# First stage of a gated stack on one core: the lower products move into the next cycle

## The reference

```python
def _smooth_quant_linear(x, w):
    s = sqrt(max(amax_over_rows(x), EPS) / max(amax_over_rows(w), EPS)); s = max(s, EPS)
    xs, ws = x / s, w * s
    x_scale = max(amax_over_columns(xs), EPS) / 127
    w_scale = max(amax_over_columns(ws), EPS) / 127
    return round(xs / x_scale) @ round(ws / w_scale).T * x_scale * w_scale.T

gate, up = split(_smooth_quant_linear(layernorm(x), fside), 2)     # upper: 512 -> 512
a = silu(gate) * up
x = x + tanh(g) * _smooth_quant_linear(a, ctx)                     # lower: 256 -> 512
```

## Time and profile before

| | |
|---|---|
| median of three runs | 1310.73 us |
| the profiled execution | 1311.2 us |
| its span | 1309.5 us |
| PE busy in the span | 1169.4 us (89%) |
| DVE busy | 831.5 us (63%) |
| ACT busy | 661.6 us (51%) |
| POOL busy | 398.6 us (30%) |
| mean granted TensorE clock | 0.964 |
| first stage ends, next one's first rows | 222.4 us |

### The profile page before, as it was taken

The page is one execution under the profiler, slowest core; times in us unless marked ns, Lnnn a source line. Parts: engine busy times, 40 slices in busy tenths (PEclk is TensorE's granted clock), DMA queues, the critical chain, the costliest instruction groups (busy, mean ns, idle before and its releaser), DMA issues.

```text
span 1309.5 us, 16528 instructions
## 1 busy us (share of the span) xinstructions
PE 1169.4 (89%) x5292; PEld 508.2 (39%) x5293; DVE 831.5 (63%) x1292; ACT 661.6 (51%) x1157; POOL 398.6 (30%) x465
## 2 busy tenths in 40 slices
...
GB/s 244 126 105 137 49 97 159 226 211 161 192 146 156 149 148 135 54 255 196 90 48 139 128 126 94 79 77 83 75 82 82 79 81 61 50 1 9 33 41 49
DMA packets 111893, 145.79 MB, mean 111 GB/s; under 512 B 25048, under 2 KB 79832, under 8 KB 111560
## 3 DMA queue, kind: packets, MB, share of 16 engines
...
## 4 chain that ended last, share of the span: by engine, by line
PE 33%; DVE 10%; issue 7%; ACT 5%; POOL 1%; DMA 1%; ACTq 0%; POOLq 0%; DVEq 0%
PE PS L2902 7%; PE PS L2803 5%; PE PS L2868 5%; PE PS L2887 4%; DVE a_top L3263 4%; PE PS L2827 3%; PE PS L2387 2%; ACT shared_w L3023 2%; ACT a_E L3023 2%; PE PS L2410 1%; PE PS L1980 1%; PE PS L2014 1%; POOL a_K L2147 1%; DMA a_rows<-f_y,l_pos 1%; PE PS L2815 0%
## 5 line engine op out<-in xcount | busy, mean ns | idle before, releaser
L3263 DVE TENSOR_REDUCE a_top<-PS 128x2 f32<-128x1024 f32 x256 | 309.3, 1222 | 88.4 <-PE PS L2887 84.9
L2868 PE MATMUL PS<-a_Q,a_K 99*128 99x512 bf16 (+1 forms) x512 | 166.2, 386 | 15.1 <-ACT a_E L3023 3.2
L3023 ACT ACTIVATE shared_w<-PS 128x512 f32<-128x512 f32 x256 | 138.8, 596 | 74.7 <-PE PS L2868 74.6
L3023 ACT ACTIVATE a_E<-PS 128x512 f32<-128x512 f32 x256 | 138.9, 596 | 63.7 <-PE PS L2868 63.5
L1498 PE MATMUL PS<-f_W,f_GT 128*128 x312 | 142.2, 599 | 0.2 <-ACT f_GT L1532 0.2
L2887 PE MATMUL PS<-a_K,a_Q 64*128 64x512 bf16 x512 | 100.5, 390 | 7.9 <-DVE a_top L3263 6.4
L1927 POOL TENSOR_TENSOR a_qf<-a_qf,a_tab 128x512 f32<-128x512 f32 x15 | 19.1, 1270 | 286.4 <-DVE a_swapped L3165 286.4
L2868 PEld LDWEIGHTS PS<-a_Q,a_K 99*128 99x128 bf16 (+1 forms) x512 | 44.1, 97 | 150.1 <-ACT a_E L3023 51.1
L1554 DVE TENSOR_TENSOR f_H<-f_SG,PS 128x256 f32<-128x256 f32 x39 | 16.4, 421 | 115.5 <-ACT f_SG L1538 115.5
L1498 PEld LDWEIGHTS PS<-f_W,f_GT 128*128 128x128 f32 x312 | 56.9, 192 | 57.9 <-issue 57.9
L2803 PE MATMUL PS<-a_xT,a_early 128*128 128x512 f32 x128 | 72.9, 667 | 2.0 <-ACT a_xT L2989 0.7
...
## 6 DMA issues: line engine op xcount, KB each, us to landing
f0r_raw<-in_L_ffn_W_dram SPq DMA_DIRECT2D x24, 512.0 KB, 5.3
...
v_units<-V SPq DMA_DIRECT2D x16, 512.0 KB, 2.9
a_V<-v_units SPq DMA_DIRECT2D x16, 512.0 KB, 3.6
...
```

The costliest lines, as they stand in the source:

```text
L2868: nc.tensor.matmul(PS[:, 4 + h % 2, :], K6[k][0:rows_, o, head // 2, kt * P:(kt + 1) * P], Q6[k][0:rows_, o, head // 2, :], start=True, st ...
L3023: nc.scalar.activation(E[step % 2][:, h, :], PS[:, 4 + h % 2, :], ACT.Exp).then_inc(exp_done, 1)
L3263: nc.vector.tensor_reduce(top[:, h - h % 2:h - h % 2 + 2, t], PS[:, 2 * pair:2 * pair + 2, :], AX.X, ALU.max).then_inc(maxed, 1)
```

## The change

The lower products and outputs of a batch move one cycle on: cycle `i` now runs the upper linear of batch `u = i`, the front of the lower linear of `d = i - 1` (turns, scales, rounded turns), and the products and outputs of batch `e = i - 2`. Within the cycle:

- TensorE no longer turns `dw` between the halves of `guw`; `dw` and `a` are turned together after the upper rows and side slot 2. The upper products follow the lower weights' rounded turns, and the lower x's rounded turns come after them. Three lower products of `e` stand behind the turns of `xh`, the fourth behind slot 1.
- VectorE takes `y` out between the ratio and the gates, runs the gates ahead of the fourth `y`, and takes the lower linear's scales in smaller pieces. 
- ScalarE runs the sines and the angles' copy at the end of a cycle, then `xqT_down`, silu and a root (of the next batch's deviation, or a spare one of a constant where there is none) ahead of the upper root. The norm of the next x moves forward, between the lower linear's steps.
- GpSimd adds a batch two cycles after its upper linear.
- `FILL` holds 8, 7, 7, 7 and 11 jobs instead of 8, 7, 7, 8 and 10, none in slot 7; the angles' job moves from slot 1 of its own cycle to slot 7 of the cycle before it.

The fourth lower product of each batch gets another bank. The diff, cut to the loops:

```diff
-        DOWN_AT = (4, 5, 6, 0)
-        LAST_AT = (0, 1, 2, 5)
+        DOWN_AT = {b: (4, 5, 6, 4) for b in range(NB - 2)}
+        DOWN_AT[NB - 2] = (4, 5, 6, 2)
+        DOWN_AT[NB - 1] = (0, 1, 2, 5)
...
+    if b >= 2:
+        add_batch(b - 2)
+    if b == NB - 1:
+        add_batch(NB - 2)
...
+def lower_products(d, tiles):
+    for t in tiles:
+        product(down, t, DOWN_AT[d][t])
...
-    u, d = i, i - 1
+    u, d, e = i, i - 1, i - 2
     pe.wait_ge(up.w_loaded, 16 * (u + 1))
     if u:
         pe.wait_ge(hs_ready, u * TB)
     turn_w(up, u, 1, 2)
-    if d >= 0:
-        pe.wait_ge(down.w_loaded, 16 * (d + 1))
-        if d:
-            pe.wait_ge(y_ready, d * TB - 2)
-        turn_w(down, d, 0, 4)
-        if d:
-            pe.wait_ge(y_ready, d * TB)
     turn_w(up, u, 0, 0)
     if u == 0:
         side.tensor_start(pe)
...
     turn_x(up, u, 1, 2)
     pe.wait_ge(up.reduced, 4 * u + 2)
     turn_x(up, u, 0, 0)
+    if e >= 0:
+        pe.wait_ge(down.xqT_ready, e + 1)
+        lower_products(e, (0, 1, 2))
     side.tensor(pe, i, 1)
-    if d >= 0:
-        turn_down_x(d)
+    if e >= 0:
+        pe.wait_ge(y_ready, e * TB + 1)
+        lower_products(e, (3,))
     s_rows(up, u, (0, 0), (1, 0))
     side.tensor(pe, i, 2)
     if d >= 0:
-        s_rows(down, d, (6, 0), (6, 256))
+        pe.wait_ge(down.w_loaded, 16 * (d + 1))
+        if d:
+            pe.wait_ge(y_ready, d * TB)
+        turn_w(down, d, 0, 4)
+        turn_down_x(d, 4)
     side.tensor(pe, i, 3)
     wsc_row(up, u, 1)
     side.tensor(pe, i, 4)
+    pe.wait_ge(up.w_shifted, u + 1)
+    turn_shifted(up.ws, 0, (2, 3), up.wqT_done)
+    if d >= 0:
+        s_rows(down, d, (6, 0), (6, 256))
     side.tensor(pe, i, 5)
+    pe.wait_ge(up.wsc_row_ready, u + 1)
+    pe.wait_ge(up.x_scaled, u + 1)
+    turn_shifted(up.ws, 1, (0, 1), up.wqT_done)
+    pe.wait_ge(up.x_shifted, u + 1)
+    for half, banks in ((0, (2, 3)), (1, (0, 1))):
+        pe.wait_ge(up.wqT_ready, 2 * u + half + 1)
+        turn_shifted(up.xs, half, banks, up.xqT_done)
     if d >= 0:
         wsc_row(down, d, 4)
-    finish_up(u)
-    side.tensor(pe, i, 6)
-    if d >= 0:
-        finish_down(d)
+        turn_down_ws(d)
     pe.wait_ge(up.xqT_ready, 2 * u + 2)
     for t in range(TB):
         product(up, t, t)
+    side.tensor(pe, i, 6)
     if d >= 0:
-        pe.wait_ge(down.xqT_ready, d + 1)
-        for t in range(TB - 1):
-            product(down, t, DOWN_AT[t])
+        turn_down_xs(d)
     side.tensor(pe, i, 7)
-    if d >= 0:
-        pe.wait_ge(hs_ready, u * TB + 1)
-        product(down, TB - 1, DOWN_AT[TB - 1])
-
...
+def bring_root():
+    nc.scalar.activation(spare_root[:], ln_eps[:], ACT.Sqrt)
...
     if d >= 0:
-        side.scalar(act, d, 7)
-        side.scalar_waves(act, d)
         silu(d)
-    side.scalar(act, i, 0)
-    side.scalar(act, i, 1)
-    root(up, u)
-    if d >= 0:
-        root(down, d)
         if u < NB - 1:
             norm_root(u + 1)
+        else:
+            bring_root()
+    side.scalar(act, i, 0)
+    root(up, u)
+    side.scalar(act, i, 1)
     side.scalar(act, i, 2)
     side.scalar(act, i, 3)
     shift_w(up, u)
     take_wsc_row(up, u, 1)
+    if d >= 0:
+        root(down, d)
     side.scalar(act, i, 4)
+    take_up_w(u, 0, 2)
     shift_x(up, u)
     if u == 0:
         norm_root(1)
+    take_up_w(u, 1, 0)
     side.scalar(act, i, 5)
-    take_up_w(u)
     if d >= 0:
         shift_w(down, d)
         take_wsc_row(down, d, 4)
-        shift_x(down, d)
-    side.scalar(act, i, 6)
+    if 0 < u < NB - 1:
+        normalize(u + 1)
     if d >= 0:
         take_down_w(d)
-        take_down_x(d)
-    if u < NB - 1:
-        normalize(u + 1)
+        shift_x(down, d)
     if u == 0:
         act.wait_ge(gates_loaded, 32)
         nc.scalar.activation(tg[:], gates[:], ACT.Tanh).then_inc(tg_ready, 1)
+        normalize(1)
+    side.scalar(act, i, 6)
+    if u < NB - 1:
+        side.scalar_waves(act, u)
+        side.scalar(act, i, 7)
+    if d >= 0:
+        take_down_x(d)
 d = NB - 1
+silu(d)
+bring_root()
 side.scalar(act, d, 7)
-silu(d)
...
-    u, d = i, i - 1
+    u, d, e = i, i - 1, i - 2
     reduce_turned(up, u, 0, 2)
-    if d >= 0:
-        reduce_turned(down, d, 0, 4)
     reduce_turned(up, u, 1, 0)
     v.wait_ge(up.x_ready, u + 1)
     reduce_turned(up, u, 2, 2)
     reduce_turned(up, u, 3, 0)
+    ratio(up, u)
+    if e >= 0:
+        take_down(e, (0, 1))
+    s_columns(up, u)
+    if e >= 0:
+        take_down(e, (2,))
+    if u == 1:
+        row_stats(3)
     if d >= 0:
         gate(d)
-    ratio(up, u)
-    s_columns(up, u)
+    if e >= 0:
+        take_down(e, (3,))
+    scale_w(up, u, 1, 0)
+    if d >= 0:
+        reduce_turned(down, d, 0, 4)
+    w_scales(up, u)
     if d >= 0:
         reduce_turned(down, d, 1, 4)
         ratio(down, d)
-    scale_w(up, u, 1, 0)
+    scale_x(up, u, 0, 0)
     if d >= 0:
         s_columns(down, d)
-    w_scales(up, u)
-    x_scales(up, u, 0, 0)
+    x_scales(up, u)
+    if 0 < u < NB - 1:
+        row_shifts(u + 1)
     if d >= 0:
         v.wait_ge(down.x_ready, (d + 1) * TB)
         scale_w(down, d, 6, 256)
         w_scales(down, d)
-        x_scales(down, d, 6, 0)
+    if u == 0:
+        v.wait_ge(x_loaded[1], 16)
+        row_stats(1)
+    take_up_x(u)
+    if u == 0:
+        row_shifts(1)
+    if d >= 0:
+        scale_x(down, d, 6, 0)
+        x_scales(down, d)
         if d == 0:
             v.wait_ge(tg_ready, 1)
         gate_scale(d)
-    if u == 0:
-        v.wait_ge(x_loaded[1], 16)
-        row_stats(1)
-    if u == 1:
-        row_stats(3)
-    if 0 < u < NB - 1:
-        row_shifts(u + 1)
-    take_up_x(u)
-    if u == 0:
-        row_shifts(1)
     take_up(u)
     if u == 0:
         row_stats(2)
-    if d >= 0:
-        take_down(d, False)
-d = NB - 1
-reduce_turned(down, d, 0, 4)
+d, e = NB - 1, NB - 2
+reduce_turned(down, d, 0, 0)
+take_down(e, (0, 1, 2))
...
-    ANGLES = 1
-    FILL = ((2, 0, 1, 0, 1, 1, 1, 2), (0, 1, 1, 1, 1, 1, 1, 1), (0, 1, 1, 1, 1, 1, 1, 1), (0, 1, 1, 1, 1, 1, 1, 2),
-(2, 1, 1, 1, 2, 1, 2, 0))
+    ANGLES = ((0, 1), (0, 7), (1, 7), (2, 7))
+    FILL = ((2, 0, 1, 1, 2, 1, 1, 0), (0, 1, 2, 1, 1, 1, 1, 0), (0, 1, 2, 1, 1, 1, 1, 0), (0, 1, 2, 1, 1, 1, 1, 0),
+(2, 1, 1, 1, 2, 2, 2, 0))
     WAVES = 17
 
```

More of the change, by code:

```diff
@@ L415, in shift_x, with take_up_w @@
                 last.then_inc(L.x_shifted, 1)
-            def take_up_w(u):
-                for half, bank in ((0, 2), (1, 0)):
-                    act.wait_ge(up.wqT_done, 2 * u + half + 1)
-                    nc.scalar.activation(up.wqT[:, 2 * half:2 * half + 2, :], PS[:, bank:bank + 2, :], ACT.Copy,
-                                         bias=-ROUNDER).then_inc(up.wqT_ready, 1)
+            def take_up_w(u, half, bank):
+                act.wait_ge(up.wqT_done, 2 * u + half + 1)
+                nc.scalar.activation(up.wqT[:, 2 * half:2 * half + 2, :], PS[:, bank:bank + 2, :], ACT.Copy,
+                                     bias=-ROUNDER).then_inc(up.wqT_ready, 1)
             def take_down_w(d):
@@ L607, in take_down @@
                     v.wait_ge(x_updated, b * TB)
-                for t in range(TB):
+                for t in tiles:
                     v.wait_ge(down.product_done, b * TB + t + 1)
-                    nc.vector.scalar_tensor_tensor(y[:, t, :], PS[:, (LAST_AT if last else DOWN_AT)[t], :], gated_scale[:, t:t + 1], down.wsc_row[:],
+                    nc.vector.scalar_tensor_tensor(y[:, t, :], PS[:, DOWN_AT[b][t], :], gated_scale[:, t:t + 1], down.wsc_row[:],
                                                    ALU.mult, ALU.mult).then_inc(y_ready, 1)
-                    if last and t:
-                        add_rows(b, t - 1)
-                if last:
-                    add_rows(b, TB - 1)
             def add_rows(b, t):
```

72 lines of the change are left out of this document (33 added, 39 removed).

## The result

Changed kernel: median 1295.87 us (1290.46 to 1297.79), run beside the kernel before at 1310.44 (1309.64 to 1312.04): ratio 0.9879, 95% interval 0.9852 to 0.9905. The forecast was 1298.7. The profiled execution was the lowest of the runs, 1290.46 (span 1288.6). Two more series gave medians of 1293.3 and 1296.3 (ratios 0.9869 and 0.9876). The change makes the kernel 1.2% to 1.3% shorter, and none of the three intervals reaches 1.

What follows compares the result with a forecast made beforehand. No engine was full; VectorE, the fullest, had 23.9 us of removable waits in the first stage. Waits -14.1, cycle 0 +1.1, tail +0.2, port +2.1 and -1.3 sum to -12.0: 1298.7 us, range 1292.5 to 1306.5.

Steps and rivals of the forecast that it cites:

- Cycle 0: +1.1: Later xs_up shift less a side product moved away: net +1.1 us, bounds 0 (TensorE at its higher level) and 4.
- some 4 us later: Cycle 0, ScalarE: the shift of xs_up stands behind more side copies and half of wqT_up, some 4 us later.
- the returned waits: New VectorE waits in cycles 2 and 3: guw's turn 2.6, dw's turn 1.5, turned x 0.3, together 4.4 us.
- the first rival: Gates beside GpSimd's angles pay the port in full, 3.5 us in each of three cycles: 1307.1 us; chance 0.08.
- The term of +2.1: Gates slowed by sharing the port with GpSimd's angles: 0.7 us in each of three cycles.
- Tail: +0.2: Turned a reduced 8.6 instead of 10.0 us after hs, an extra side job costing 1.7: +0.2 us (-1.4 to +1.7).
- the root's wait: VectorE's old wait of 2.70 us in each cycle for ScalarE's root; covered in cycles 2 and 3, 0.7 left in cycle 1.
- the wait on the products: VectorE's old waits of 6.45 us in cycle 2 and 4.66 in cycle 3 for the upper products, forecast to go.
- the cover of the root: Cycles 2 and 3: VectorE's two y run until the root is there, with 0.5 us to spare.
- the loop's terms: Slower rival: sines waiting for GpSimd's angles close a loop of 34.5 us, against a cycle of 41; 1316 us, chance 0.05.
- TensorE's lower level: Rival: turns and first products at 1.2 GHz behind waits, 3 us uncovered in each of three cycles: 1307.7 us; chance 0.08.
- ScalarE's loads: Rival: three table loads ahead of the root, each 1.28 us dearer, +10.4 us: 1309.1, no change; chance 0.03.

Runs made afterwards that it cites:

- e1: The changed kernel run again without any edit; median 1293.3 us, ratio 0.9869 to the kernel before.
- e12: The changed kernel run once more without any edit, on the chip of the three kernels before it; median 1296.3 us, ratio 0.9876.
- e6: The changed kernel with the old table of side jobs in cycle 0; median 1301.2 us, ratio 0.9903 to the kernel before.
- e10: The changed kernel with GpSimd's angles held until the cycle's gates are done and the tail's gates ahead of the lower outputs; 1293.2 us, ratio 0.9861.
- e7: The changed kernel with the tail's four gates ahead of all lower outputs; median 1296.3 us, ratio 0.9879 to the kernel before.
- e2: The kernel before with only the upper products moved ahead of the lower turns of ws and xs; median 1316.8 us, ratio 1.0066.
- e5: The kernel before with upper products ahead of the lower turns, and the root and its table ahead of slot 1's copy; 1316.5 us, ratio 1.0040.
- e4: The changed kernel with the turns of the lower xs put back ahead of the upper products; median 1313.3 us, ratio 1.0024 to the kernel before.
- e9: The changed kernel with lower products and outputs put back into their own cycle; median 1301.6 us, ratio 0.9915 to the kernel before.

## Why the prediction was right, and where its terms were not

The sum of -12.0 stands against -16.9 in the profiled stage (-13.5 and -19.8 in e1 and e12) and -14.6, -16.4 and -16.4 in the medians. That the total is so close is in part luck: cycle 0 was forecast 4.5 us too long and the tail 3.8 too short, and these two errors cancel. By its own split (waits, gates and small operations of each cycle together), predicted and measured in the first profile:

- Cycle 0: +1.1, measured -3.4. The step that failed is the shift of `xs_up`, "some 4 us later": ScalarE began it at 33.69, not 33.39, 1.0 us further behind its scale, as the further copies fitted into the idle 1.09 and 0.36 ahead of it. With half of `wqT_up` taken before it, TensorE turned xs at 36.28 instead of 38.00, and the product of 2.72 between turn and products was gone. e6 shows that the side-job table had no part in it. A second part was not in the sum: 1.4 of the 3.4 us is busy time of VectorE. The angles' copy now stands behind the root, GpSimd starts its angles at 21.77 instead of 20.94, and four small operations that took 0.44, 0.43, 0.32 and 0.72 take 0.17, 0.21, 0.17 and 0.16. TensorE also stayed at its higher level, the case for which the prediction had put 0 (granted clock 1.00 in 28 to 41 us, 0.79 before). Cycle 0 is the largest error. TensorE before, then ScalarE and TensorE after:

```profile
38.00 2.82 PE L283 MATMUL PS<-identf,xs_up 128*128 128x128 f32 x16 [2.13 <-ACT wqT_up L420]
```

```profile
33.69 2.55 ACT L417 ACTIVATE xs_up<-xs_up,inv_scale_up 128x512 f32<-128x512 f32 x4
```

```profile
36.28 2.19 PE L291 MATMUL PS<-identf,xs_up 128*128 128x128 f32 x16 [0.96 <-ACT xs_up L417]
```

- Cycle 1: -4.9, measured -5.3. Cycle 2: -5.2, measured -6.8: the returned waits are 3.65 + 1.17 = 4.8 (forecast 4.4), but `hs` is 0.6 shorter and the gates are only 0.4 longer, time that the wait for dw would have taken.
- Cycle 3: -3.2, measured -5.5: waits of 2.1 instead of 4.4. The gates took 3.35, 1.95 more than alone, over half of the 3.5 that the first rival had for a cycle, and VectorE spent in them the time in which it would have waited for dw; e10 gives the time back as a wait. The term of +2.1 was near in size (0 + 0.4 + 1.95) and wrong as a cost: it was added to the waits, and all but 0.35 of it lay inside one of them.
- Tail: +0.2, measured +4.0 (+3.2 in e12, +2.6 in e1). Turned `a` was to be reduced 8.6 us behind `hs`; it was 11.1 (176.70). The term missed that the gates meet GpSimd's additions (3.56 instead of 1.42): in e7, with the gates ahead of the additions, `a` was reduced 8.8 us behind `hs`. The wait of 2.40 for dw, now turned behind `hs`, costs nothing against before: it stands in e7 too (2.41), and the old tail waited 3.38 for the fourth `y` instead. From that reduction to the stage's end it took 28.8 instead of 25.9: 3.0 more, not the 1.7 of the extra side job (the last wait on `y` is 9.46 instead of 7.12), at a granted clock of 0.87 against 0.96 before; in e10, at 1.00, it is still 2.4 more. The Trainium skill's page "SBUF — State Buffer" (Who interferes with whom) says that a VectorE instruction with two SBUF inputs contends with a GpSimd one that reads; the trace agrees there, the gates take 3.56 beside the additions and 1.43 ahead of them in e10. VectorE after:

```profile
168.01 1.23 DVE L557 TENSOR_REDUCE amax_down<-PS 128x2 f32<-128x1024 f32 x1 [2.40 <-PE PS L265]
...
176.70 1.23 DVE L557 TENSOR_REDUCE amax_down<-PS 128x2 f32<-128x1024 f32 x1 [1.35 <-PE PS L271]
...
196.03 1.41 DVE L626 SCALAR_TENSOR_TENSOR y<-PS,gated_scale,wsc_row_down 128x512 f32<-128x512 f32 x2 [9.46 <-PE PS L296]
```

Of the signs, the root's wait, the wait on the products and the lengths of the cycles came as written (39.6 to 41.4 us); ahead of the first `amax_up` 3.65 stood in cycle 2 instead of 2 to 3, ahead of `amax_down` nothing in cycle 3, and the last side copy ended at 201.2 instead of near 205. Small slips of the working: from 131.55 to 135.97 it is 4.4 us and not 4.3, the cover of the root is 0.7 by its own terms and not 0.5, the loop's terms add to 34.7 and not 34.5; none moves the forecast.

Of the rivals, TensorE's lower level did come, in all three cycles of e1 (0.7, 2.2 and 1.0 us longer than e12's) and none of e12, at a smaller price than the rival's 3 each. ScalarE's loads stayed at 1.28, with the next activation 0.01 behind (92.43, then 93.72): no drain. GpSimd waited 11.3 and 5.1 us for ScalarE's tables, so its loop was far from closing. The two large terms, products ahead of the lower xs and outputs in the next cycle, were right as mechanisms: the waits of 6.45, 4.66 and 2.70 went. They are not parts that can be added up. The first alone in the old order makes the kernel longer (e2), also with the root covered (e5); undone in the new order it takes the whole gain along (e4), the second undone takes a third (e9). So the move of the outputs needs the products' place, but two thirds of the gain stand without the move.

Open: e9 is still 13.0 us shorter in its stage than before, of which cycle 0 is 5.6 (some 2.2 of it the first turned x, which came early in that profile) and cycle 1 5.3; the rest of ScalarE's and TensorE's new order was not taken apart. Nor was what decides whether TensorE falls to its lower level behind a wait of 1.44.
